# Quantisation grids of a fused attention and fp8 feed-forward kernel: absolute values taken unscaled, the scale applied on VectorE, and a new instruction order

## The reference

```python
# attention: scores come from ctx_1024, and the (layer-normed) x is mixed over its last axis
q = ctx @ Wq.T + bq;  k = ctx @ Wk.T + bk
x1 = x + layernorm(x) @ softmax(q @ k.T, -1).T
# feed-forward, every operand rounded to fp8 e4m3 on a grid of its own row
xr = layernorm(x1);  qx = fp8(xr / row_scale)
g = qx @ fp8(w_gate_rows).T;  u = qx @ fp8(w_up_rows).T      # both times their scales
t = silu(g) * u;  qt = fp8(t / row_scale)
out = x1 + qt @ fp8(w_down_rows).T                           # reordered by down_reorder_index
```

## Time and profile before

| | before |
|---|---|
| time, median of 3 | 88.43 us |
| profiled execution: time / span | 88.46 / 86.6 us |
| TensorE (matmul) busy | 70.0 us, 81% of the span |
| VectorE busy | 72.1 us, 83% |
| ScalarE busy | 55.9 us, 65% |
| POOL busy | 52.8 us, 61% |
| mean granted TensorE clock | 0.961 of full speed |
| read from memory / written | 5.44 / 1.41 MB, almost all reads in the first 17 us |

### The profile page before, as it was taken

One profiled execution on the slowest core, in us unless ns is written; L12 is line 12 of the kernel. 1 busy time (PEld: TensorE's weight loads), 2 busy tenths in 40 slices (PEclk: granted clock), 3 DMA queues, 4 the chain that ended last, 5 costly groups with the idle time before them and its releaser, 6 DMA issues. The chain is left out here.

```text
span 86.6 us, 1408 instructions
## 1 busy us (share of the span) xinstructions
PE 70.0 (81%) x415; PEld 54.6 (63%) x415; DVE 72.1 (83%) x172; ACT 55.9 (65%) x109; POOL 52.8 (61%) x66
## 2 busy tenths in 40 slices
PE   5959694979945699983899998798879987483998
PEld 5732344558624588652898878685867965251587
DVE  1045489998999999998999999999999989999340
ACT  0603799877989798999869854479170973652200
POOL 4000007949995798586887889986571867626900
PEclk9999999999999858999999999999999999999759
DMA  1899999300000000000000010600000010110331
GB/s 9 314 409 394 292 402 395 117 0 0 0 0 8 0 8 0 0 0 0 30 30 30 30 38 15 181 4 0 0 0 0 0 64 0 61 64 4 121 121 61
DMA packets 5239, 6.94 MB, mean 80 GB/s; under 512 B 656, under 2 KB 3600, under 8 KB 5232
## 3 DMA queue, kind: packets, MB, share of 16 engines
q1 hardware_dynamic: 4464, 5.45, 18.3%
q10 hardware_dynamic: 576, 1.05, 3.2%
q0 software_dynamic: 192, 0.36, 1.4%
HBM read 5.44 MB, written 1.41 MB: 79 GB/s over the span
## 5 line engine op out<-in xcount | busy, mean ns | idle before, releaser
L405 POOL TENSOR_TENSOR q_t<-sum_t,grid_t 128x704 bf16<-128x704 f32 x7 | 10.7, 1530 | 5.1 <-DVE sum_t L908 3.6
L384 POOL TENSOR_TENSOR sum_w<-sum_w,grid_w 128x512 f32<-128x512 f32 x5 | 5.8, 1163 | 11.6 <-DVE grid_w L776 11.6
L1197 PE MATMUL up_ps<-w_hi,qxT 128*128 128x352 f32 x32 | 10.7, 337 | 2.1 <-DVE t_sb L882 2.1
L1197 PE MATMUL gate_ps<-w_hi,qxT 128*128 128x352 f32 x32 | 10.8, 338 | 1.9 <-issue 1.8
L1197 PE MATMUL up_ps<-w_lo,qxT 128*128 128x352 f32 x32 | 10.3, 322 | 0.0
L1197 PE MATMUL gate_ps<-w_lo,qxT 128*128 128x352 f32 x32 | 10.3, 322 | 0.0
L908 DVE SCALAR_TENSOR_TENSOR sum_t<-t_sb,s_t,grid_t 128x704 f32<-128x704 f32 x7 | 9.1, 1294 | 0.5 <-issue 0.4
L590 ACT ACTIVATE grid_t<-t_sb,s_t 128x704 bf16<-128x704 f32 x7 | 6.2, 881 | 4.3 <-DVE s_t L767 4.3
L597 ACT ACTIVATE tT<-bank_b 128x768 bf16<-128x768 bf16 x7 | 5.6, 804 | 4.8 <-PE bank_b L1227 4.8
L818 DVE TENSOR_REDUCE peak_w<-wup_sb 128x4 f32<-128x1024 f32 x3 | 3.6, 1216 | 5.4 <-DMA wup_sb<-w_gate_up_dram 5.4
L1197 PEld LDWEIGHTS up_ps<-w_hi,qxT 128*128 128x128 f32 x32 | 6.0, 188 | 3.2 <-issue 2.3
(11 more groups left out here) (110 smaller groups left out, 190.4 us busy)
## 6 DMA issues: line engine op xcount, KB each, us to landing
wup_sb<-w_gate_up_dram ACTq DMA_DIRECT2D x4, 256.0 KB, 4.9
xT<-x_t_dram SPq DMA_DIRECT2D x2, 512.0 KB, 8.9
x_sb<-x_dram SPq DMA_DIRECT2D x4, 256.0 KB, 10.1
out_dram<-o_sb SPq DMA_DIRECT2D x8, 128.0 KB, 1.7
wdn_sb<-w_down_dram SPq DMA_DIRECT2D x1, 704.0 KB, 9.4
ctx_sb<-ctx_t_dram SPq DMA_DIRECT2D x2, 256.0 KB, 5.2
wup_sb<-w_gate_up_dram SPq DMA_DIRECT2D x2, 256.0 KB, 5.4
wdnT_in_order<-wdnT_order SPq DMA_DIRECT2D x1, 320.0 KB, 3.0
```

Source lines behind the costliest of these rows:

```text
L384: nc.gpsimd.tensor_tensor(sum_w[:, k], sum_w[:, k], grid_w[:, k], ALU.add).then_inc(sum_w_done[k], 1)
L405: nc.gpsimd.tensor_tensor(q_t[:, i % 2], sum_t[:, i % 2], grid_t[:, i % 2], ALU.subtract)\
L1197: last = nc.tensor.matmul(ps[:, h, 0:IH], qxT[:, b, c, j * P:(j + 1) * P].bitcast(F32R), w[:, c, a, h * IH:(h + 1) * IH].bitcast(F32R), st ...
```

## The change

Four things change.

1. ScalarE no longer multiplies by the row scale when it takes absolute values. `scale_x`, `scale_down`, `scale_t` and `scale_last` become `absolute_x`, `absolute_down` and `absolute_t`, which write |v| times the constant 2^20 into new bf16 tiles `abs_x`, `abs_d`, `abs_t`. They wait for the data alone and no longer for the scale. `absolute_x` is one instruction of 512 columns where there were two of 256; `absolute_t(7)` is one of 704 where there were two.
2. The grid operation on VectorE reads that tile and a scale of one number per partition (`s`, float32), multiplies, and takes the maximum. For x it becomes two instructions of 256 columns per batch, as the two row tiles have scales of their own. It now writes another tile than it reads, and `grids_t(i)` waits for `q_t_done[i - 2]`, as the buffer is still read until then.
3. The output tile `o_sb` is now a view of the memory of `x_sb`.
4. The order of the calls on all four compute engines is new.

```diff
@@ ScalarE
-            def scale_t(i):
-                act.wait_ge(s_t_done, i + 1)
+            def absolute_t(i):
+                act.wait_ge(t_done, i + 1)
                 if i >= 2:
-                    act.wait_ge(q_t_done[i - 2], 1)
-
-                nc.scalar.activation(grid_t[:, i % 2], t_sb[:, i % 2], ACT.Abs, scale=s_t[:, i:i + 1])\
-                    .then_inc(scaled_t, 1)
+                    act.wait_ge(grid_t_done, i - 1)
+                nc.scalar.activation(abs_t[:, i % 2], t_sb[:, i % 2], ACT.Abs, scale=GRID)\
+                    .then_inc(abs_t_done, 1)
...
@@ VectorE
-                return nc.vector.tensor_scalar(grid, grid, LEAST, 2.0 ** GRID_SHIFT, ALU.max, ALU.mult)
+            def scaled_grids(grid, absolute, s):
+
+                return nc.vector.tensor_scalar(grid, absolute, s, LEAST * GRID, ALU.mult, ALU.max)
...
             def grids_x(b):
-                dve.wait_ge(scaled_x, b + 1)
-                grids(grid_x[:, b]).then_inc(grid_x_done, 1)
+                dve.wait_ge(abs_x_done, b + 1)
+                dve.wait_ge(s_x_done, b + 1)
+                for j in range(LT):
+                    i = LT * b + j
+                    last = scaled_grids(grid_x[:, b, j], abs_x[:, b, j], s_x[:, i:i + 1])
+                last.then_inc(grid_x_done, 1)
...
             def grids_t(i):
-                dve.wait_ge(scaled_t, i + 1)
-                grids(grid_t[:, i % 2]).then_inc(grid_t_done, 1)
+                col = slice(i, i + 1)
+                dve.wait_ge(abs_t_done, i + 1)
+                dve.wait_ge(s_t_done, i + 1)
+                if i >= 2:
+                    dve.wait_ge(q_t_done[i - 2], 1)
+                scaled_grids(grid_t[:, i % 2], abs_t[:, i % 2], s_t[:, col]).then_inc(grid_t_done, 1)
...
-        o_sb = sb("o_sb", [P, T, N])
+        o_sb = x_sb[:, :, :, :].rearrange("p (b j) n -> p (b j) n")
```

More of the change, by code:

```diff
@@ L173, in build @@
         y_sb = sb("y_sb", [P, 2, N])
-        o_sb = sb("o_sb", [P, T, N])
+        o_sb = x_sb[:, :, :, :].rearrange("p b j n -> p (b j) n")
         bank_a, bank_b = bank("bank_a"), bank("bank_b")
@@ L519, in centre_x1, with absolute_x @@
                 last.then_inc(xc2_done, 1)
-            def scale_x(b):
+            def absolute_x(b):
                 act.wait_ge(xc2_done, b + 1)
-                act.wait_ge(s_x_done, b + 1)
-                for j in range(LT):
-                    i = LT * b + j
-                    last = nc.scalar.activation(grid_x[:, b, j], xc2[:, b, j], ACT.Abs, scale=s_x[:, i:i + 1])
-                last.then_inc(scaled_x, 1)
+                nc.scalar.activation(abs_x[:, b], xc2[:, b], ACT.Abs, scale=GRID).then_inc(abs_x_done, 1)
             def evac_qxT(b):
@@ L912, in grids_last @@
             def grids_last(h):
-                dve.wait_ge(scaled_last, h + 1)
-                step(grids(grid_t[:, LAST, part(h)]), ("grid_last", h))
+                dve.wait_ge(abs_t_done, T)
+                dve.wait_ge(s_t_done, T)
+                dve.wait_ge(q_t_done[T - 3], 1)
+                step(scaled_grids(grid_t[:, LAST, part(h)], abs_t[:, LAST, part(h)], s_t[:, T - 1:T]),
+                     ("grid_last", h))
             def add_grid_last(h):
```

264 lines of the change are left out of this document (129 added, 135 removed).

## The result

The change makes the kernel faster, and by more than forecast: 81.51 us (median of 4 runs, 81.0 to 83.5) against 88.63 for the kernel before on the same chip, a ratio of 0.917 (95% interval 0.911 to 0.923).

A forecast was written before the change was run, and what follows sets the result against it. The prediction took VectorE to bound the kernel, partly standing still behind POOL, with `keep_busy` ending the span. From 88.46 us it took off 2.5 (up to the last part), 1.15 (tail) and 0.6 (`keep_busy`): 84.2 us, range 82.0 to 87.4.

The forecast's parts named there:

- The mechanism: Hidden stage: VectorE sets the pace and its two-input sums stand still behind POOL's SBUF reads, 4.7 us of collisions.
- The collisions: Hidden stage, first `t_sb` to last part: the new order cuts VectorE's stalls behind POOL from 4.7 to 1.9 us.
- three ties: Behind tiles 1, 5 and 6, POOL's queue and VectorE's free work last equally long: 0.2 us of collision each.
- `add_residual` pair: Two POOL residual sums behind tiles 2, 4, 3 meet the grid of tile 5: 0.4 us of collision.
- everything fits: Rival: no ties lost in the hidden stage and the scale operand free, 1.5 us less, 82.6 us; chance 0.1.
- The start: Up to the first `t_sb`: 1.5 us gained, 1.0 us of added or moved work, so 44.3 instead of 44.76.
- The grid operation: VectorE's grid with a scale per partition keeps its fast mode: 0.06 us more each, 11 times, 0.7 us.
- The rival of 91.4 us: The scale operand takes the grid's fast mode away on VectorE: 7.2 us more, 91.4 us; chance 0.1.
- worth 0 by itself; it only frees the order: Unscaled absolute values on ScalarE: the shorter round trip gains 0, as VectorE never idled for a ScalarE grid.
- The tail: Last part to end of last `down`: 1.8 us instead of 2.96 with `down(6)` moved ahead, 1.15 gained.
- The end: Behind the last `down`: `keep_busy` falls from twelve to ten matmuls, 3.82 to 3.2 us, 0.6 gained.
- The rivals of both sides: Collisions stay at 4.7 us, 87.0 us, chance 0.15; nothing but added work, 88.2, 0.05; fast mode lost, 91.4, 0.1.

The follow-up runs named there:

- first pair: Profiles of the kernel before (88.46 us) and of the unchanged kernel after, profiled a second time (82.12 us).
- with 10 warming rounds: TensorE does 10 instead of 6 matmuls on zeros before the first projection: kernel after 81.44 us, kernel before 87.3 us.
- writes-only run: Kernel before, with POOL writing zeros for tiles 0 to 6 instead of computing `q_t`, so it reads nothing there: 83.34 us against 87.23.
- order runs: Kernel after with the old order everywhere (89.29 us), only up to the first gates (83.63 us), or only behind them (86.15 us).
- e_residual_later: Kernel after with 10 warm-up matmuls, four y buffers, row 3's residual sum later on POOL, row 5's on VectorE: 81.34 us.
- e_before_warm10: Kernel before with 10 instead of 6 warm-up matmuls on TensorE: 87.3 us, ratio 0.979.
- after_again: Kernel after, unchanged, run again for a second profile: 81.74 us against 88.33 for the kernel before, ratio 0.930.
- e_old_order: Kernel after's new operations in the old order of every engine: 89.29 us, ratio 1.017 to the kernel before.
- e_new_start: Kernel after with the new order up to the first gates and the old order from there: 86.15 us, ratio 0.980.
- e_scaled_new_order: Kernel after with the old operations (ScalarE multiplies by the scale, output in own memory) in the new order, `scale_x(0)` later: 93.43 us.
- e_old_pool: Kernel after with POOL's list from the second `subtract_x` on in the old order: two runs 87.1 us, two 92.0.

## Why the prediction was right, and where it was not

The first pair of profiles mixes two things: less work and waiting, and how TensorE's clock and start fell out in two executions. The two profiles with 10 warming rounds both start fast and both keep the clock at the end. By their marks:

| change of the piece, us | forecast | first pair | with 10 rounds |
|---|---|---|---|
| start to the first `t_sb` | -0.46 | -1.23 | -1.24 |
| to the end of the last part | -2.0 | -3.03 | -3.14 |
| to the end of the last `down` | -1.15 | -1.18 | -0.54 |
| to the end of the span | -0.6 | -0.86 | +0.02 |
| in all | -4.2 | -6.3 | -4.9 |

- **The mechanism: right.** VectorE set the pace and stood still behind POOL's reads; the new order takes that away. The writes-only run and the order runs show it.
- **The collisions: mis-sized, 1.9 us where 0.7 were left.** I gave 0.2 to each of three ties and 0.4 to the `add_residual` pair. All of them are free (`sum_t` 951 ns in the mean). Only the last parts still collide: the 320-column sum 0.81 against about 0.57 (an estimate of the prediction), and `q_t` 0.90 against the 0.49 that `e_residual_later` measured, so 0.65 where I had 0.9. With the 31.0 us of work that makes 31.65, and 31.90 were measured; the step that failed is the price of the ties. The rival "everything fits" (82.6 us, chance 0.1) came nearest: its half on the ties came true, its half on a free operand did not.
- **The start: 0.46 forecast, 1.23 measured, and the reason was wrong.** The sum had 1.5 gained, most of it by filling a gap, and 1.0 added by more and moved work. Both terms failed. "VectorE idled 1.45 us until the scores were there" was TensorE's slow start in that execution and no property of the order: with a fast start on both sides the first residual comes only 0.48 us sooner (20.34 to 19.86), of which the 0.26 us wait for `rstd` and `s_w` (0.17 us where it took 0.49) are a part. And from there to the first `t_sb`, where I had 0.35 us more than before (23.15 to 23.5), it is 0.76 less (23.33 to 22.57). Two pieces of that can be seen: the sums of the down weights no longer stand still (`sum_d` 946 ns where it took 1109, twice), and a wait of 0.4 us for ScalarE's `w_hi`, behind a fall of TensorE's clock in `e_before_warm10`. The rest was not taken apart. In `after_again` the same stretch is 23.34, which looks like my 23.5, but 0.69 of it is a wait for TensorE while its granted clock was 0.50 (40 to 42 us); in the first profile after, where the clock held, it is 22.56.
- **The grid operation: right.** The fast mode stays. 0.078 us more at 704 columns (I said 0.06), 0.29 for a 256-column half. The rival of 91.4 us is out. The whole cost of the operations is 1.5 us by the ratio of `e_old_order`, as in my sum; its interval reaches from 0.6 to 2.5.
- **Absolute values "worth 0 by itself; it only frees the order": right** on both sides. With the old order they bring nothing (89.29), and without them the new order takes 93.43 us where it takes about 81.5 with them. (For x it is one instruction less per pair on ScalarE, not two.)
- **The tail: right in the number, and half of it for another reason.** 1.78 came for 1.8, but 0.65 of the 1.18 us gained is the clock of the profile of before, whose last six matmuls took 1.57 us; where the clock held, the old order took 2.31 us and the gain is 0.54. I had seen the slow matmuls and left the clock open (0.45 to 0.75 us for three of them), but the sum has no clock in it. The new end seems to help the clock: with the old end the last six matmuls were slow in three of five profiles (`before`, `e_old_order`, `e_new_start`), with the new one in one of eleven (`e_scaled_new_order`). Why was not shown.
- **The end: right by 0.25, for the wrong reason.** "The last store is no later than that" is false: the store ends the span, 0.65 us behind `keep_busy`. The 0.86 gained are the 24 slow records of `keep_busy` in the profile of before (0.159 us each; 20 take 0.125 each now). With the clock held the piece was 3.08 us before and is 3.10 after: two matmuls on zeros fewer bring nothing.
- **What the sum had no term for: the clock.** Of 40 runs of the kernel before, recorded beside the experiments, 2 had a mean clock of 1.00, and none of the 6 of `e_before_warm10`; of the 14 of the kernel after (ten of them with 10 warming rounds) it was 8. The profiles with 10 rounds give 4.9 us, the medians of all runs 7.1. So part of the measured gain seems to be fewer falls of the clock. How much, and why the new order has fewer, was not shown.
- **The rivals of both sides: wrong.** Collisions that come back (87.0) is what `e_new_start` and `e_old_order` show, not the change; the order as a whole did not lose its gain elsewhere.
- **"VectorE idle for more than 1 us with TensorE or POOL as releaser"** did not come. But POOL is nearer to being the bound than my sum, which followed VectorE, could tell: `e_old_pool` needs only POOL's old list to lose 5 us.

## What to carry to other kernels

A busy share can hide a stall: compare the mean duration of a shape with its shortest, and look at what the neighbour engine was reading. When two engines exclude each other, plan both lists as pairs, with single-input work of the one beside each reading instruction of the other. A step that removes a dependency may bring nothing until the order is rewritten around it, so it has to be judged with that order. And before a gap or a slow piece of one profile is put into a sum, look in a second execution whether it is there; here the gap at the start was TensorE's in that execution, and the slow end came in some executions of the same order and not in others.
